# First loads on one queue, both first means together, tile 0 in chunks of one and three, and idle products on ones

## The reference, cut to what matters

```python
x = hidden                                   # (8, 256, 512): 16 tiles of 128 tokens x 512
xn = (x - mean(x)) / sqrt(var(x) + 1e-5)
q = xn @ Wq.T + bq                           # only every fourth head is used: 8 heads x 128
sig = elu(q) + 1
retrieved = (sig @ M) / (sig . z + 1e-6)     # per head
out = x + repeat(retrieved, 4) @ Wo.T + (xn @ (w_int8 * w_scale) + b)
```

## Time and profile before

| | |
|---|---|
| median of 3 runs | 237.94 us (237.75 to 238.29) |
| the profiled execution's own time | 237.95 us |
| its span, first to last instruction | 236.1 us |
| PE busy | 232.5 us, 98% of the span |
| DVE, ACT, POOL busy | 174.0, 125.2, 107.4 us |
| first q product on PE starts | 6.08 us into the span |

### The profile page before, as it was taken

The page is one execution under the profiler, slowest core; times in us unless marked ns, Lnnn a source line. Parts: engine busy times, 40 slices in busy tenths (PEclk is TensorE's granted clock), DMA queues, the critical chain, the costliest instruction groups (busy, mean ns, idle before and its releaser), DMA issues.

```text
span 236.1 us, 3421 instructions
## 1 busy us (share of the span) xinstructions
PE 232.5 (98%) x1037; PEld 188.4 (80%) x1037; DVE 174.0 (74%) x275; ACT 125.2 (53%) x285; POOL 107.4 (45%) x117
## 2 busy tenths in 40 slices
PE   8999999999999999999999999999999999999995
PEld 3688788888888788888888888888888888888895
DVE  2989999897589987997858859585667879362511
ACT  4845358687298386585547253654637445630300
POOL 1029437856932356558350442524045598480000
PEclk9999999999999999999999999999999999999999
DMA  6999999999590144471727272431134456879521
GB/s 227 389 412 414 356 250 254 224 212 218 133 278 17 41 95 130 96 180 48 175 89 178 72 196 77 91 104 39 52 94 97 136 135 159 191 189 182 193 98 44
DMA packets 24081, 38.76 MB, mean 164 GB/s; under 512 B 5440, under 2 KB 13248, under 8 KB 22912
## 3 DMA queue, kind: packets, MB, share of 16 engines
q1 hardware_dynamic: 18816, 26.10, 33.7%
q0 software_dynamic: 3808, 11.14, 24.5%
q10 hardware_dynamic: 1440, 1.31, 1.9%
HBM read 25.95 MB, written 4.19 MB: 128 GB/s over the span
## 4 chain that ended last, share of the span: by engine, by line
PE 98%; DVE 0%; issue 0%
PE attn_ps L876 14%; PE attn_ps L878 14%; PE attn_ps L877 13%; PE q_ps L876 10%; PE q_ps L878 10%; PE q_ps L877 10%; PE dense_ps L876 6%; PE dense_ps L878 6%; PE dense_ps L877 6%; PE dense_ps L967 2%; PE q_ps L916 1%; PE q_ps L904 1%; PE q_ps L911 1%; PE attn_ps L916 1%; PE attn_ps L904 1%; PE attn_ps L911 1%
## 5 line engine op out<-in xcount | busy, mean ns | idle before, releaser
L489 ACT ACTIVATE s<-s,rden 128x128 f32<-128x128 f32 x128 | 39.2, 390 | 39.3 <-DVE rden L707 37.6
L341 POOL TENSOR_TENSOR e_and_sz<-s,z_b 128x512 f32<-128x512 f32 x32 | 41.7, 1340 | 39.6 <-DVE den L703 39.6
L876 PE MATMUL attn_ps<-P_hi,aT_hi 128*128 128x512 f32 (+1 forms) x136 | 53.0, 389 | 0.0
L878 PE MATMUL attn_ps<-P_hi,aT_lo 128*128 128x512 f32 (+1 forms) x136 | 52.2, 384 | 0.0
L877 PE MATMUL attn_ps<-P_lo,aT_hi 128*128 128x512 f32 (+1 forms) x136 | 52.1, 383 | 0.0
L876 PE MATMUL q_ps<-WqT_hi,xT_hi 128*128 128x512 f32 x104 | 40.7, 391 | 0.0
L878 PE MATMUL q_ps<-WqT_hi,xT_lo 128*128 128x512 f32 x104 | 40.5, 389 | 0.0
L877 PE MATMUL q_ps<-WqT_lo,xT_hi 128*128 128x512 f32 x104 | 40.5, 389 | 0.0
L691 DVE SCALAR_TENSOR_TENSOR q_ps<-q_ps,rstd,bq_b 128x512 f32<-128x512 f32 x28 | 21.0, 752 | 17.6 <-PE q_ps L878 17.6
L876 PEld LDWEIGHTS attn_ps<-P_hi,aT_hi 128*128 128x128 f32 x136 | 25.6, 188 | 6.1 <-issue 0.6
L878 PEld LDWEIGHTS attn_ps<-P_hi,aT_lo 128*128 128x128 f32 x136 | 25.6, 188 | 5.2
(11 more groups left out here) (96 smaller groups left out, 356.1 us busy)
## 6 DMA issues: line engine op xcount, KB each, us to landing
x<-in_WoT POOLq DMA_DIRECT2D x6, 1024.0 KB, 11.0
x<-in_b POOLq DMA_DIRECT2D x16, 256.0 KB, 4.4
out<-x SPq DMA_DIRECT2D x15, 256.0 KB, 2.4
x<-in_x SPq DMA_DIRECT2D x14, 256.0 KB, 3.6
xT<-in_xT SPq DMA_DIRECT2D x13, 256.0 KB, 3.8
aT<-s SPq DMA_DIRECT2D x104, 32.0 KB, 2.3
MT<-s SPq DMA_DIRECT2D x72, 32.0 KB, 1.9
x<-in_WoT SPq DMA_DIRECT2D x2, 1024.0 KB, 13.3
```

The costliest lines, as they stand in the source:

```text
L341: nc.gpsimd.tensor_tensor(sz_eps[:, :, h * D // 2:(h + 1) * D // 2].rearrange("p g (j c) -> p j g c", j=2), by_quarter(sbuf_s[:, t % SRING ...
L489: last = nc.scalar.activation(a_g, a_g, ACT.Copy, scale=rden[:, t % 2, g:g + 1])
L876: nc.tensor.matmul(out, x_hi, w_hi, start=start, stop=False)
L878: return nc.tensor.matmul(out, x_lo, w_hi, start=False, stop=stop)
```

## The change

Six edits, all in the first ten microseconds. (1) The two loads that ACT issued, the first piece of WqT and tile 1's xT, are issued by SP; tile 1's xT is SP's second load. (2) `sum_chunks(1)` stands right behind `sum_chunks(0)` on DVE, and `mean_of_columns(1)` right behind `mean_of_columns(0)` on PE. (3) Tile 0 is centred and split as one chunk and three chunks, not two and two. (4) The lo part of tile 0's first chunk is made ahead of the first weight piece's lo part. (5) PE's first passes are in another order. (6) The idle products read a constant tile of ones that is there from the program's start, wait for nothing, and are 7 of 512 columns and 3 of 128 ahead of the means and 2 of 512 behind them (8 and 3 of 512 before, the 3 after the first mean).

```diff
+        def first_chunks(j):
+            return [slice(0, 1), slice(1, K)][j]
...
             load_xT(0)
+            load_xT(1)
+            load_wq_half(0, 0)
             load_wq_half(0, 1)
             load_wq_half(1, 0)
...
             nc.scalar.activation(table_loaded[:], warm[:, 0:1], ACT.Copy)
-            act.dma_start(WqT_raw[:, 0, halves(0)], WqT_d[0, 0][:, halves(0)]).then_inc(wq_half_in[0], 16)
-            act.dma_start(xT[:, 1, :, :].rearrange("p k r -> p (k r)"), xT_d[1]).then_inc(xT_in[1], 16)
             copy_wq_hi(0, 0)
             copy_first_xT_hi(0)
...
-                nc.vector.tensor_tensor(xT[:, 0, chunks(j), :], xT[:, 0, chunks(j), :],
-                                        mean_in(0).unsqueeze(1).to_broadcast([P, K // 2, P]),
+                nc.vector.tensor_tensor(xT[:, 0, first_chunks(j), :], xT[:, 0, first_chunks(j), :],
+                                        mean_in(0).unsqueeze(1).to_broadcast([P, 1 if j == 0 else K - 1, P]),
                                         ALU.subtract).then_inc(xc_by_dve, 1)
...
             elif t == 0:
-                    pe.wait_ge(xT_lo_ready, 1 + k // 2)
+                    pe.wait_ge(xT_lo_ready, 1 + min(k, 1))
...
-            def keep_busy(n):
+            def keep_busy(n, width=HID):
                 for i in range(n):
-                    nc.tensor.matmul(dense_ps[:], warm[:], warm[:].unsqueeze(1).to_broadcast([P, 4, P]), start=True, stop=True)
-
-            pe.wait_ge(warm_set, 1)
-            keep_busy(8)
+                    nc.tensor.matmul(dense_ps[:, 0:width], nc.const_aps.tensor(1.0, [P, P], BF16),
+                                     nc.const_aps.tensor(1.0, [P, width], BF16), start=True, stop=True)
+
+            keep_busy(7)
+            keep_busy(3, P)
             mean_of_columns(0)
-            keep_busy(3)
+            mean_of_columns(1)
+            keep_busy(2)
             hi_hi(0, 0, 0)
+            lo_hi(0, 0, 0)
+            hi_hi(0, 1, 0)
+            lo_hi(0, 1, 0)
             hi_lo(0, 0, 0)
-            hi_hi(0, 1, 0)
-            lo_hi(0, 0, 0)
-            lo_hi(0, 1, 0)
-            mean_of_columns(1)
+            hi_hi(0, 0, 1)
+            hi_lo(0, 1, 0)
+            hi_hi(0, 1, 1)
             for h in range(2):
-                hi_hi(0, h, 1)
                 lo_hi(0, h, 1)
-            hi_lo(0, 1, 0)
             hi_hi(0, 0, 2)
             lo_hi(0, 0, 2)
             hi_lo(0, 0, 1)
```

More of the change, by code:

```diff
@@ L434, in copy_first_xT_hi @@
                 act.wait_ge(xc_by_dve, j + 1)
-                nc.scalar.activation(xT_hi[:, 0, chunks(j), :], xT[:, 0, chunks(j), :], ACT.Copy
+                nc.scalar.activation(xT_hi[:, 0, first_chunks(j), :], xT[:, 0, first_chunks(j), :], ACT.Copy
                                      ).then_inc(xT_hi_ready, 1)
@@ L642, in split_first_xT_lo @@
                 dve.wait_ge(xT_hi_ready, j + 1)
-                nc.vector.tensor_tensor(xT_lo[:, 0, chunks(j), :], xT[:, 0, chunks(j), :],
-                                        xT_hi[:, 0, chunks(j), :].bitcast(F32), ALU.subtract).then_inc(xT_lo_ready, 1)
+                nc.vector.tensor_tensor(xT_lo[:, 0, first_chunks(j), :], xT[:, 0, first_chunks(j), :],
+                                        xT_hi[:, 0, first_chunks(j), :].bitcast(F32), ALU.subtract).then_inc(xT_lo_ready, 1)
             def split_xT_lo(t):
@@ L734, in _ @@
             sum_chunks(0)
+            sum_chunks(1)
             center_first(0)
             center_first(1)
+            split_first_xT_lo(0)
             split_wq_lo(0, 0)
-            split_first_xT_lo(0)
-            sum_chunks(1)
             split_wq_lo(0, 1)
@@ L901, in hi_hi @@
                 elif t == 0:
-                    pe.wait_ge(xT_hi_ready, 1 + k // 2)
+                    pe.wait_ge(xT_hi_ready, 1 + min(k, 1))
                     pe.wait_ge(wq_hi_ready, 2 * k + h + 1)
```

## The result

The changed kernel takes 238.84 us (median of 8 runs, 238.51 to 239.68), the kernel before 237.94 (8 runs beside it, 237.75 to 238.29): ratio 1.0044, interval 1.0035 to 1.0053. It is slower by 0.9 us. Forecast were 237.4 us and faster. The profiled execution took 238.61 us, against 237.95 before, so 0.66 of the 0.9 us can be looked at in the traces.

The account below looks back on a forecast made before the run. PE was taken as the bound, busy 232.5 of 236.1 us; with s = 0.3 its unbroken stretch starts at 9.12, not 9.69, so 237.95 - 0.57 = 237.4 us, range 237.05 to 238.2.

Parts of the forecast that it names:

- s: Early loads: time by which every load from the second place on lands earlier; taken as 0.3 us, between 0 and 0.55.
- Lower end s = 0: Early loads land no earlier than before; first pass needing piece (1, 0)'s lo part at 9.45, gain 0.24 us.
- the hole: Slow stretch between the first two load landings, worth 0.43 to 0.6 us; stays: chance 0.28, closes wholly: 0.20.
- the rule of the Trainium skill's page: Early loads: issuing from several engines saves sequencer time alone, so moving two loads closes no hole; 237.7 us.
- What is late next: PE's wait at 26.50 for tile 3's lo part: its DVE chain can come earlier by 0.27 plus s.
- a gain of 0.57 us: Start of PE's unbroken stretch: the pass needing piece (1, 0)'s lo part moves from 9.69 to 9.12.
- It lets the gain through in each case: Wait at 26.50: DVE's chain comes earlier by 0.57 us for s = 0.3, 0.27 for s = 0, enough for the gain.
- The sum of tile 1 in DVE's idle time: DVE from 4.20 to 5.15: tile 1's sum moves there, taking 0.66 us off the busy stretch.
- the arithmetic of the chunks: Tile 0's centring on DVE: paces 0.20 us for 128 columns and 0.47 for 384, the sum unchanged.
- the idle products at nothing: PE's start: idle products on ones end by 4.05, worth under 0.1 us and hidden behind DVE's sum of tile 1.
- a longer wait at 26 us: Sign of being wrong: PE's wait near 26 us grows and takes back the gain.
- The late clock: Rival: PE idles around the early means, its full clock comes later, up to 238.7 us; chance 0.15, 0.11 slower than 238.4.

Follow-up runs that it names:

- (4): Changed kernel with tile 1's xT issued by ACT as its first load, everything else by SP with the first weight piece second: 238.34 us (12 runs).
- changed with x(1) behind: Changed kernel with the load of x of tile 1 moved behind the int8 weights and their scales: 239.70 us (6 runs).
- x(3) ahead: Kernel before with the load of x of tile 3 put between the int8 weights and their scales: 238.68 us (5 runs).
- (1): Changed kernel with the first weight piece issued by ACT again, tile 1's xT still second on SP: 239.51 us (11 runs).
- (3): Changed kernel with x of tile 2 as SP's third load, ahead of the first weight piece: 240.76 us (1 run).
- the kernel before with x(1) behind: Kernel before with the load of x of tile 1 moved behind the int8 weights and their scales: 237.70 us (12 runs).
- both attempts: Changed kernel with x of tile 1 behind the scales, 239.70 us (6 runs); with x of tiles 0 and 1 behind them, 239.10 us (5 runs).

## Why the prediction was wrong

**"Call s the time by which every load from the second place on lands earlier ... Lower end s = 0".** This is the step that failed. Second place was as hoped, by 4.34 against 4.45 forecast. From the third place on s was negative, 6.02 against 5.39: -0.63, and -0.73 at the int8 weights. The bound rested on the hole being a fault of the second queue, or else staying as it was. I had two readings of one hole and no row to choose by, and none in which it grew. The runs show that the step goes with the third load, on one queue (5.5 to 6.4 us) and in (4) on two; why is open. With the rule of the Trainium skill's page "DMA: Bandwidth & Descriptors", that the issuing engine changes nothing but the issue time, s was to be 0; the runs differ from that sum too: the loads' edit alone cost 0.97 us (237.94 to 238.91). They do not refute the rule, since the edit changed the order and the moment of the issues along with the engine.

**"What is late next".** The prediction saw the wait at 26.50 and traced it to the right engine, but took DVE's busy time for work: "DVE has run to it without idle time from 15.56". Two of the operations in that stretch were held, `scale_w` of 2.52 us (1.22 alone) and a `wd_lo` of 2.17 us beside GpSimd's centring of a tile (1.22 the first time). The stretch hangs on GpSimd's `scale_w`, that is on the landing of the scales. Over all 16 profiled executions (both kernels and the 14 experiments), 237.49 to 240.76 us long, the time of the execution less the end of `xT_lo(3)` is 211.42 to 211.80 us: before 237.95 - 26.46 = 211.49, changed 238.61 - 27.16 = 211.45, changed with x(1) behind 239.54 - 28.04 = 211.50, x(3) ahead 239.09 - 27.30 = 211.79. That one end goes with the time to within 0.4 us. It can be the cause only where PE waited for it, in 13 of the 16 (0.30 to 0.57 us in PEld's rows). In (1), (3) and the kernel before with x(1) behind PE had no gap there: in (1) and (3) PE was late itself, by the slow passes and in (3) by the late piece, and DVE's centring of tile 2 waited for PE's mean (0.90 and 0.63 us).

So a gain of 0.57 us in the first 10 us would not have got through by itself, had it come: PE would have stood at the same gate at 26.50, waiting longer, unless the scales landed earlier too. With s = 0.3 for every load they would have, by 0.3; as `xT_lo(3)` ended 10.23 us after GpSimd's start, 0.3 us and not 0.57 is my estimate of what that s was worth. "It lets the gain through in each case" had the wrong chain.

**How the loss is made up.** In the changed kernel PE reached the gate at 27.21 - 0.53 = 26.68, before at 26.50 - 0.30 = 26.20. The late first products are 0.48 us of it, of which 0.18 show beyond the old gate at 26.50; the gate does the other 0.53, if these two single executions stand for the rest. That the late gate alone is enough is shown (x(3) ahead: 0.7 us, first products on time). That the changed kernel would come down to about 238.2 with the gate lifted is not: both attempts lifted the scales and hit the lock.

**What was right.** The sum of tile 1 in DVE's idle time; the arithmetic of the chunks (128 columns take 0.29 us, a pace of 0.20, as by the straight line); the idle products at nothing; and a longer wait at 26 us was named among the signs of being wrong. The late clock, given a chance of 0.15, cost nothing in the profiled execution but two idle products at the slow pace (0.84 us for both, from 5.73), ahead of a wait of 0.34 us for ACT. Two of the 8 runs of the changed kernel took 239.42 and 239.68; whether these had the late clock, as (1) had, or something else, no profile shows.

**The best kernel** of the study is the one before with x(1) behind the scales, 237.70 us; by its interval (0.9982 to 1.0005) that may be no gain at all.

## What to carry to other kernels

An unbroken row of work on an engine can still be waiting: compare each operation's duration with the same form elsewhere on the page before calling a chain its own bound, and where a two-input operation on VectorE stands beside GpSimd, expect its end to be GpSimd's. A change to the first loads of a queue moves every load behind it, so follow the last of them that has a deadline (here the scales, 10 us on), not only the one that was meant. And before counting a gain ahead of a gate, find which event sets the gate: here the scales' landing set it in most executions, PE's own lateness or a held operation in others.

## What the runs showed of the hardware

- On one queue at the start of the kernel the second load of 256 KB lands 0.6 to 1.2 us after the first, and the third another 1.1 to 2.3 us later, whichever tensor it is. By 14 us the loads stand 0.6 us earlier with the two loads on ACT's queue (means 13.9 and 14.5). The cause is open.
- VectorE operations with two inputs in SBUF, started while GpSimd runs such a one, end 0.54 to 0.56 us (512 columns) or 1.07 to 1.09 us (1,024 columns) after GpSimd's end, whenever they start: 0.69 us becomes 2.87, 1.22 becomes 3.45. The profile shows the hold as busy time. The one-input statistics are not held.
- PE's clock can fall again. In (3) PE had its full clock before it waited 2.05 us for the late piece, and the first passes behind the wait start 0.43 apart again, until 11.23; the timeline of (3), its one run:

```profile
5.43 0.60 PE L970 MATMUL dense_ps<-const-bfloat16-1.0 128*128 128x512 bf16 x2
8.08 0.80 PE L907 MATMUL q_ps<-WqT_hi,xT_hi 128*128 128x512 f32 x1 [2.05 <-ACT xT_hi L440]
...
10.38 0.63 PE L907 MATMUL q_ps<-WqT_hi,xT_hi 128*128 128x512 f32 x1
10.80 0.63 PE L919 MATMUL q_ps<-WqT_lo,xT_hi 128*128 128x512 f32 x1
11.23 0.50 PE L907 MATMUL q_ps<-WqT_hi,xT_hi 128*128 128x512 f32 x1
```

The two idle products there took 0.60 us for both, as at 2.4 GHz; the two of (1) took 1.06. Windows of (3), the granted clock being the third number from the end:

```profile
7.25:8.00 0.75, 0.00 (x0) 0.00 (x0) 0.00 (x0) 0.75 (x3) 0.00 (x0) 1.00 0.96 369
8.75:9.50 0.75, 0.75 (x3) 0.59 (x2) 0.75 (x3) 0.75 (x3) 0.00 (x0) 0.50 1.09 415
```
